# A graph network's edge work in two halves: the first half's src-ordered stage runs beside the second half's scatter

## The reference

```python
# layer 0 (row = src, col = dst)
msg = relu((x @ W_m1.T + b_m1)[row] + (x @ W_m2.T + b_m2)[col] + edge_attr @ W_me.T + b_me)   # 96 wide
msg = relu(msg @ W_net.T + b_net)
agg = segment_max(msg, row)
x   = layernorm(x + x @ W_o1.T + b_o1 + agg @ W_o2.T + b_o2)
# layer 1
h   = gelu(concat(x[src], x[dst]) @ eW1 + eb1) @ eW2 + eb2
x   = layernorm(x + x + mlp(concat(x, segment_sum(h, dst))))
```

## Time and profile before

| | us |
|---|---|
| median of 3 runs | 3815.32 (3814.55 to 3818.74) |
| profiled execution, from its first to its last instruction (span) | 2838.6 |
| median less that span | 976.7 |
| PE, PEld, DVE, ACT, POOL busy in the profiled execution | 2320.7, 2014.7, 2036.0, 1000.7, 1860.7 |

### The profile page before, as it was taken

One profiled execution on the slowest core, in us unless ns is written; L12 is line 12 of the kernel. 1 busy time (PEld: TensorE's weight loads), 2 busy tenths in 40 slices (PEclk: granted clock), 3 DMA queues, 4 the chain that ended last, 5 costly groups with the idle time before them and its releaser, 6 DMA issues. The chain is left out here.

```text
span 2838.6 us, 89638 instructions
## 1 busy us (share of the span) xinstructions
PE 2320.7 (82%) x22430; PEld 2014.7 (71%) x22431; DVE 2036.0 (72%) x9631; ACT 1000.7 (35%) x2286; POOL 1860.7 (66%) x2595
## 2 busy tenths in 40 slices
PE   7778888888888888799999988876677777777777
PEld 6578777777777777477777766766677666777777
DVE  8678777777777777777787877566666666666666
ACT  7334333333333333144444447222222222222225
POOL 1047777777777777654444437677777777777774
PEclk9789999999999999899999998899999999999999
DMA  5021111111111111188888973222222222222221
GB/s 187 29 57 47 45 45 45 45 45 45 45 45 45 45 45 48 35 218 228 226 226 225 227 194 78 54 54 54 54 54 54 53 54 54 54 55 54 55 53 46
DMA packets 582003, 236.10 MB, mean 83 GB/s; under 512 B 512256, under 2 KB 553772, under 8 KB 581676
## 3 DMA queue, kind: packets, MB, share of 16 engines
q1 hardware_dynamic: 298020, 98.53, 15.3%
q0 software_dynamic: 52736, 93.92, 11.6%
q10 hardware_dynamic: 231176, 42.79, 7.5%
HBM read 142.39 MB, written 98.65 MB: 85 GB/s over the span
## 5 line engine op out<-in xcount | busy, mean ns | idle before, releaser
L1041 POOL DMA_INDIRECT edge_in_src_order<-u,place x784 | 756.6, 965 | 259.9 <-issue 185.2
L1714 POOL DMA_INDIRECT a_rows<-src_table,idx x782 | 742.2, 949 | 248.8 <-issue 237.9
L1791 PE MATMUL ps_h<-a_rows,ident 128*128 x1664 | 237.8, 286 | 247.3 <-SPq L1723 185.4
L1791 PEld LDWEIGHTS ps_h<-a_rows,ident 128*128 128x128 f32 x1664 | 202.6, 192 | 278.9 <-issue 278.7
L1411 POOL COPY m_s<-m 128x144 f32 x832 | 234.0, 325 | 244.0 <-PE ps_pre L1458 242.9
L1831 ACT ACTIVATE h<-ps_h 128x512 f32<-128x512 f32 x208 | 124.2, 597 | 743.6 <-PE ps_h L1796 653.9
L1760 DVE TENSOR_SCALAR ohd_f<-iota_b,dloc_c 128x128 f32<-128x128 bf16 x832 | 199.1, 312 | 209.8 <-PE ps_s L1805 204.1
L1434 DVE TENSOR_TENSOR_SCAN top<-same,top,ps_net 96x512 f32<-96x512 bf16 x207 | 264.1, 1276 | 97.9 <-PE ps_net L1465 97.6
L1335 ACT COPY u<-ps_u 128x384 f32<-128x384 f32 x196 | 93.7, 478 | 604.1 <-DMA edge_in_src_order<-u,place 581.7
L1258 PE MATMUL ps_u<-we_s,attrT 128*128 128x384 f32 x392 | 173.8, 525 | 158.9 <-ACT u L1335 158.9
L1748 DVE TENSOR_TENSOR hsumT<-hsumT,ps_s 128x128 f32 x832 | 238.2, 286 | 84.4 <-DVE deg L1750 1.8
(11 more groups left out here) (357 smaller groups left out, 5400.8 us busy)
## 6 DMA issues: line engine op xcount, KB each, us to landing
u_in<-edge_in_src_order SPq DMA_DIRECT2D x208, 192.0 KB, 3.4
running_max<-row ACTq DMA_DIRECT2D x208, 192.0 KB, 4.2
rowt<-src_row SPq DMA_DIRECT2D x208, 130.0 KB, 3.7
key_b<-edge_keys ACTq DMA_DIRECT2D x832, 1.5 KB
edge_in_src_order<-u,place POOLq DMA_INDIRECT x784, 2.2
a_rows<-src_table,idx POOLq DMA_INDIRECT x782
edge_attributes<-in_edge_attr SPq DMA_DIRECT2D x8, 784.0 KB, 12.0
attr_in<-edge_attributes SPq DMA_DIRECT2D x196, 32.0 KB, 1.9
```

The source lines that it names most:

```text
L1041: pool.indirect_dma_start(u_d, bass.IndirectOffsetOnAxis(place[:, u, j:j + 1], 0), ur[:, u, j, :], None).then_inc(sent[u], 16)
L1714: pool.indirect_dma_start(a_rows[:, 4 * u + j, :], None, a_d, bass.IndirectOffsetOnAxis(idx[:, u % 4, j:j + 1], 0)).then_inc(got[u % 4], 16)
L1791: m.matmul(ps_h[k][:, j, :], ident[:], a_rows[:].rearrange("p c d -> p (c d)")[:, bass.ds(slot[j], D)], start=(j == 0), stop=False, skip_g ...
```

## The change

The edges are split into two halves of 98 groups. Each half has its own ranks and its own region of `u_d` and `s_d` (111 groups each, 222 together, where there were 208).

- **Tables block.** Only the first half's histogram is counted there (49 turns). The block borders of dst come from a search and not from 50 sign passes on ACT. `m2` is made for blocks of 112 nodes (56 of them, not 49), and its last 16 partitions hold `w_e`. The keys are no longer bounced through DRAM. The wide matmuls with ones are f16 and not f32.
- **Scatter stage.** The attributes are loaded transposed into partitions 112 to 127 of `dstT`, so that one matmul against `m2` adds the edge part: L1238 and L1258 go, and the ACT copy of the attributes with them. The 12 one-hots become 3 `tensor_tensor` operations. `ps_eq`, `ps_cnt`, `ps_pre`, `ps_net` and `ps_top` have one bank each while both stages run. The sends read a ring of 16 groups (`ring_u`, `ring_p`) in place of 4 buffers. All 200 turns are straight-line code.
- **Hooks.** The second half's histogram, both halves' marks and slot rows, the ranks of the second half, the offset tables of layer 1, and zeros for the second half of `s_d` are done at given turns of the scatter stage.
- **Turns.** From turn K0 = 98 + 16 - 4 = 110 to turn 199 each engine runs one group of the scatter stage and one of the src-ordered stage. SP waits, before the first group of each half, until all sends of that half have landed. The rest of the src-ordered stage, 132 groups, follows alone.
- **Staging.** The `m1` limbs are staged by DVE (two chunks) and ACT (two chunks) and no longer by POOL. `oh`, `m1_s`, `msg` and `top` have 2 buffers, not 4.
- **Gathers.** The last rows are gathered for each half while the stage runs (98 indirect transfers), and DVE takes the maximum of the two halves. `x1T` is overlaid by the ring and loaded again after the last send.

```diff
-def pipeline(eng, count, stages, cool=0, unroll=4):
+def pipeline(eng, last, stages, done=0, cuts=(), cool=0, unroll=4, early=8):
...
+RG = 16
...
+                GB = 2 * GS
+                K0 = CS + RG - 4
+                C_STEPS = CG + 4
+                KS = C_STEPS - K0 + 1 & -2
...
+                def pick_bank(banks, i, u):
+                    return banks[0] if isinstance(i, int) and i < KS else banks[u % 2]
...
+                        def load_u(i, u, n):
+                            if isinstance(i, int) and i in (0, GS):
+                                groups_sent(sp, CS if i == 0 else CG)
...
+                        for i in range(CG):
+                            wait(pool, sent[i % 4], 64 * (i // 4))
+                            pool.wait_ge(place_ready, i + 1)
+                            pool.wait_ge(u_ready, i + 1)
+                            for j in range(4 * (i % RG), 4 * (i % RG) + 4):
+                                pool.indirect_dma_start(u_d, bass.IndirectOffsetOnAxis(ring_p[:, j:j + 1], 0),
+                                                        ring_u[:, j, :], None).then_inc(sent[i % 4], 16)
...
+                            for table, to, size in ((lo_f, ohlo[:, u], SL), (dloc, ohd[:, i % 2], BD), (hi_f, ohhi[:, i % 2], HIW)):
+                                last = v.tensor_tensor(to, bcast(table[:, now].rearrange("p (c a j) -> p c a j", a=1, j=2), P, 2, size, 2),
+                                                       bcast(iota_2[:, 0:size].unsqueeze(1), P, 2, size, 2), ALU.is_equal)
...
+                        def stage(i, u, n):
+                            wait(dve, pre_ready, i - 1)
+                            at = offsets(nc, mybir.EngineType.DVE, sf_row[0:1, bass.ds(4 * i, 2)], (NB - 1) * 3 * F)
+                            for j in range(2):
+                                last = v.tensor_copy(m1_s[:, u % 2, j, :], m1[:, bass.ds(at[j], 3 * F)])
...
+                        order = [("d", 4, scan), ("c", 3, advance), ("c", 3, same_step), ("c", 3, coarse), ("c", 4, across_steps), ("c", 3, fine),
+                                 ("c", 4, put), ("c", 0, onehot), ("d", 0, onehot_b), ("d", 0, stage)]
...
+                        order = [("c", 1, turn), ("d", 3, net), ("c", 3, product), ("d", 5, turn_top), ("c", 3, count), ("c", 2, equal), ("d", 1, pre_u)]
...
+                        for now in range(C_STEPS):
+                            for kind, lag, work in order:
+                                step([(kind, lag, work)], kind, CG if kind == "c" else GB, now - (0 if kind == "c" else K0))
+                            hooks(now)
+                        pipeline(pe, GB, [(lag, work) for kind, lag, work in order if kind == "d"], done=C_STEPS - K0, early=KS + 4)
```

More of the change, by code:

```diff
@@ L27 @@
 C_HI, C_LO, C_DST = 0, 1, 2
+BD = 112
 CH = 7
@@ L43, in sizes @@
     return nb, q, ns
-def pipeline(eng, count, stages, cool=0, unroll=4):
+def pipeline(eng, last, stages, done=0, cuts=(), cool=0, unroll=4, early=8):
     most = max(lag for lag, _ in stages)
-    warm = most + 2 * unroll
-    warm += -warm % unroll
-    end = (count - cool) // unroll * unroll
+    ends = [0, *cuts, last]
     def turn(k, u):
@@ L58, in turn, with straight, step @@
             n, v = k + (u - lag) // unroll, (u - lag) % unroll
-            if isinstance(k, int) and not 0 <= unroll * n + v < count:
+            i = unroll * n + v
+            if isinstance(k, int) and not 0 <= i < last:
                 continue
-            stage(unroll * n + v, v, n)
-    def straight(first, last):
-        for t in range(first, last):
+            stage(i, v, n)
+    def straight(lo, hi):
+        for t in range(lo, hi):
             turn(t // unroll, t % unroll)
[L66 to L70, removed]
+    for a, b in zip(ends, ends[1:]):
+        lo = max(done, a + most + (early if a == 0 else 0))
+        lo += -lo % unroll
+        hi = (b - (cool if b == last else 0)) // unroll * unroll
+        if hi - lo < 2 * unroll:
+            continue
+        straight(done, lo)
+        with eng.Fori(lo // unroll, hi // unroll) as k:
             for u in range(unroll):
                 turn(k, u)
-    straight(end, count + most)
+        done = hi
+    straight(done, last + most)
+def step(stages, of, count, t):
+    for kind, lag, stage in stages:
+        i = t - lag
+        if kind == of and 0 <= i < count:
+            stage(i, i % 4, i // 4)
 def offsets(nc, engine, row, last):
@@ L1436, in scan, with border_rows @@
                                                  ALU.mult, ALU.max).then_inc(top_ready, 1)
-                        pipeline(dve, G, [(4, scan), (0, onehot)])
+                        def border_rows(q):
+                            wait(dve, x_turned, q - 2)
+                            for j in range(min(4, ND - 1 - 4 * q)):
+                                b = 4 * q + j + 1
+                                last = v.tensor_scalar(oh_x[:, q % 3, j, :], iota_b[:, 0:BD], split_l[:, b:b + 1], None, ALU.is_equal)
+                            last.then_inc(x_oh, 1)
@@ new lines, in _ @@
+                        order = [("d", 2, first), ("c", 1, turned), ("c", 3, rows), ("d", 5, rows_out_of), ("d", 6, store), ("d", 0, stage)]
+                        for q in range(BX):
+                            act.wait_ge(x_turned, q + 1)
+                            wait(act, x_ready, q - 1)
+                            k = min(4, ND - 1 - 4 * q)
+                            s.copy(dstT_x[:, q % 2, 0:k].rearrange("p j e -> p (j e)"), ps_split[q % 2][0:BD, 0:P * k]).then_inc(x_copied, 1)
+                        act.wait_ge(x_chain, ND)
```

2422 lines of the change are left out of this document (1312 added, 1110 removed).

## The result

The changed kernel takes 3759.8 us (median of 4 runs, 3746.5 to 3778.0) where the kernel before takes 3816.7 (4 runs, 3814.6 to 3818.7): ratio 0.9855, 95% interval 0.983 to 0.9881. That is faster, as forecast, and clear of noise, but by 57 us and not by 186, and 3760 lies above the stated range of 3530 to 3710.

What follows compares the result with a forecast made beforehand. POOL's transfers were taken to bound the scatter stage and layer 1's edges, PE the src-ordered stage. Terms -166, -30 and +10 made -186: span 2653, time 3630 us; likeliest range 3590 to 3680, wider range 3530 to 3710.

Steps and rivals of the forecast that it cites:

- the frame: Whole kernel: span 2838.6 us, median 3815.3; the 976.7 us taken as outside the span are carried over unchanged.
- Rival 4: Whole kernel: time outside the span isn't constant; 3565 us if runs slow proportionally, 3545 if sends are slower; chance 0.24.
- Tables block: Before the first send: fewer histogram turns and no key bounce gain 30 us (10 to 55), first send at 164.
- First half sent: Scatter stage: POOL finishes the first half's 98 groups 506 us after s, the first send.
- Scatter turns: Scatter stage before sharing: POOL's four sends set 5.06 us a turn, with PE at 3.15 and DVE at 2.6.
- Shared turn: Turns with one scatter and one src-ordered group: 5.8 us each (5.3 to 6.6), including a stall behind `rowt`.
- Rival 1: Shared turns: slower at 6.6 us each, 70 us more, 3700 us, but the change still gains; chance 0.17.
- Lone group: Src-ordered groups run alone after the shared turns: 2.42 us each (2.32 to 2.8), 319 us in all.
- Stage: Scatter, slot rows and src-ordered stage together: from 1504 to 1338 us after the first send, gain 166.
- Node stage: Node stage: taking the gathers out gains nothing; last store, last gather, maximum and engines' meeting add 10 us.
- Rival 2: Shared turns: DVE's port use stretches sends from 1.266 to 1.39 us and POOL bounds; 3600 to 3640 us, chance 0.13.
- Rival 3: Shared turns: over 7.9 us because PE waits for DVE's scan behind a late `rowt`; slower than before, 3865; chance 0.06.

Runs made afterwards that it cites:

- g0: Kernel before with layer 1's 782 indirect POOL gathers replaced by SyncE loads of fixed rows, on a slow chip: 3215.9 us, ratio 0.8505.
- s0: Kernel before with its scatter stage written out turn by turn on all five engines, not as a loop, on a slow chip: 3798.2 us, ratio 0.9952.
- experiment 3: Changed kernel with no shared turns (K0 = 196, not 110), on a slow chip: 3885.8 us, ratio 1.028 to the kernel before.
- a1: Changed kernel with only three waits held at 1 or more, several runs on a slow chip: 3726.4 us against 3780.9 for the kernel before, ratio 0.9866.
- experiment 6: Changed kernel with half 1's 49 node gathers each issued beside one of half 2's, not in one run, on a slow chip: 3719.4 us, ratio 0.9751.
- b0: Kernel before run again with only two waits on loaded values held at 1 or more, on a quick chip: 2838.0 us.
- a0: Changed kernel run again with only three waits on loaded values held at 1 or more, on a quick chip: 2663.0 us.
- k196: Changed kernel with K0 = 196, so the src-ordered stage starts only after all scatter groups, on a slow chip: 3885.8 us, ratio 1.028.
- m0: Changed kernel with the two halves' node gathers issued in pairs instead of 49 in one run, on a slow chip: 3719.4 us, ratio 0.9751.
- g1: Kernel before with layer 1's indirect gathers replaced by plain transfers of fixed rows, still issued by POOL, on a slow chip: 3127.9 us, ratio 0.8195.
- g2: Kernel before with two of each group's four layer 1 gathers replaced by SyncE loads of fixed rows, on a slow chip: 3152.2 us, ratio 0.8261.
- p3: m0 with a 384-wide POOL memset ahead of each layer 1 gather, on a slow chip: 3433.2 us, ratio 0.9079 to the kernel before.

## Why the prediction was wrong

**The step that failed is the frame.** The prediction says: "I make the sum in the span's time and carry the 976.7 us outside it over unchanged." Those 977 us lie inside the stages, and nearly all of them where POOL issues indirect transfers. For the kernel before on slow chips: scatter stage 1396 against 995 (g0's window), layer 1 1448 against 978, and the node stage, whose 49 gathers are one run, 142 (s0, last scan to first layer-1 gather) against 88: together some 925. The rest is spread. There was a warning: no run had given a time and a span of the same execution, and a median and a span that differ by a third need not be of like executions. With the frame fell what was read from the quick trace and carried over: a scatter turn of 5.06 us is 7.1 to 7.5 on a slow chip, and a shared turn of 5.8 is 7.9 to 8.2.

The Trainium skill, "Runtime: NRT & Kernel Launch", section "The ~15µs preamble/postamble breakdown", puts some 9 to 15 us around a kernel; that was nearer than my frame. The runs show 1.7 to 2.0 us between an execution's time and its span.

**Rival 4** was the nearest of the cases, and had the wrong victim. It priced a slower send at 977 / 1615 = 0.6 us each and concluded that PE then has more room, gain 270. It is right that the loss goes with the indirect transfers. But their own time is the same on both kinds of chip (0.95 us busy, 0.30 behind it); it is PE, DVE, ACT and SP that stand still. So PE gets no more room there: on slow chips a shared turn takes 7.9 to 8.2 us, the lighter scatter turn stays at 7.2 to 7.5, and the sharing hides 159 us (experiment 3) where the rival had 209.

**Where the gain went on a slow chip**, from g0 and a1 on one chip (first send, last src-ordered scan, end of span): before 194.4, 2108.4 and about 3779; after 141.1, 2077.4 and 3718.5. Prologue 53 us gained; the two stages 1914.0 against 1936.3, 22 lost where a quick chip gains 131; behind them 1671 against 1641, 30 gained. Together 61; the medians differ by 54.5, since a1's profiled run is its fastest. The 153 us between the 131 and the -22 lie in two places. Up to the last send the changed kernel takes 1506 us where before takes 1395, on the quick chip 1012 where before takes 993: 92, of which 34 fall in the first half's turns, lighter as they are, and 58 in the second's, most of them shared. From there to the last scan it takes 432 where before takes 521, on the quick chip 356 where before takes 507: 61, and the run of 49 gathers, which stood in the node stage before, costs about that there (experiment 6). The node stage is 51 shorter for it (142 in s0, 91 in a1).

**The sum itself**, against the quick chip (b0 and a0 together, by windows and the starts of scans):
- *Tables block, 30 forecast (10 to 55).* First send 196.5 to 141.8: 55. Undersized, at its bound.
- *First half sent at s + 506.* The 393rd send begins at s + 506.4. Right to the 4 us that I had put on top for landing and load.
- *Scatter turns, 5.06.* 5.17 us before sharing. Right: POOL's pace, DVE and PE below it.
- *Shared turn, 5.8 (5.3 to 6.6).* 76 scans in 418.5 us are 5.5 each, with PE 442 of 444 us busy, while POOL's groups go on at 5.16 from the ring's lead. PE bounds it; the stall behind `rowt` that I added is small, 14 us of waits in 390. Rival 1 is out.
- *Lone group, 2.42 (2.32 to 2.8).* 125 scans in 344.8 us are 2.76: PE is 0.91 busy and DVE 0.81, and they wait for each other. Undersized by 0.34 x 132 = 45 us, the largest error of the sum. Whether the 2 buffers in place of 4 or the staging on DVE and ACT is behind it wasn't tested. The sum also counts 87 + 21 + 111 = 219 of the 222 groups; three more at 2.42 are 7 us.
- *Stage, 166.* 1498.1 against 1366.9 from first send to last scan: 131.
- *Node stage, -10.* 86 us before, 92 after: -6.
- Sum: 55 + 131 - 6 and 5 lost in layer 1 and the last stage, 175 against 186. That they lie so close is in part luck: the tables gave 25 more than forecast and the stage 35 less.

**Rival 2** (DVE's marks and copies stretch the sends). Sends in the shared turns of the quick chip:

```profile
L1299 POOL DMA_INDIRECT edge_in_src_order<-ring_u,ring_p x303 | 298.8, 986 | 92.5 <-issue 82.1 <-DMA edge_in_src_order<-ring_u,ring_p 7.0 <-ACT ring_u L1699 1.8
```

986 ns against 963: 23 ns more and not the 128 of the earlier trace rows, and the turns before sharing show 986 too. **Rival 3** (a shared turn over 7.9) did happen, on slow chips, but not by its mechanism of a late `rowt`: PE and the others stand still; and as the kernel before is slower there too, it didn't decide the sign.

What stays open: what differs between the two kinds of chip, and that it is the chip; what in an indirect transfer holds up the other engines, and on which of them it falls first; k196 on a quick chip. It isn't the loading of code: layer 1 of s0 has 11 packets on the queues for instructions from 2300 to 3600 us, and that of b0, with no stop, 11 from 1800 to 2700. The ratio of a1 to m0 compares two slow chips, each with its own runs of before.

## What to carry to other kernels

If a profiled execution and the timed ones differ by more than a few us, find out first that they are the same thing: compare span, granted clock and stages of one execution with its own time, and make no sum before that. Where a stage issues many indirect transfers from POOL, time its kernel on several chips: a change that moves other engines' work beside such transfers was worth 6.2% on one kind and 1.4% on the other. There, runs of such transfers 1.25 us apart cost more than pauses do; with plain transfers, with pairs and a pause (1.99 us from one to the next on average), or with an even 1.58 us, layer 1 got shorter. On the quick kind the even spacing only costs: 3341 against 2838 us for the kernel before, and 3130 against 2663 for the changed one.

## What the hardware showed that I had not expected

- In five of the seven sets of runs (the result's and six more, these on six chips) PE, DVE, ACT and SP stand still while POOL issues indirect transfers one behind the other; in the other two there is hardly such a gap. The transfers themselves take 0.95 us of POOL, and their last packet ends 2.2 us after their start, on both kinds of chip. The Trainium skill, "SBUF — State Buffer", section "SBUF: two separate sides", says that compute and DMA can't slow each other ("A DMA cannot be slowed by a compute op, and vice versa"). g1's plain transfers agree with it. Beside the gathers, at the same 64 KB each, the other engines do stand still; that it happens at the SBUF isn't shown, so this needn't contradict the page, but a reader of it would not expect the stops.
- The stops come in steps. Of the pairs of L2059's weight loads that follow each other in layer 1 (after, 2300 to 3500 us), 71 begin 0.6 to 0.8 us apart, 51 begin 1.3 to 1.5 apart, 23 begin 2.1 to 2.2 apart and 27 at another distance over 0.4; on the quick chip none reaches 0.4.
- The granted clock goes with the stops: 0.74 to 0.77 in layer 1 and in the changed kernel's turns that aren't shared, 0.83 in the scatter stage of before, 0.90 in the shared turns, and 0.98 to 1.00 in layer 1 without them (g0, g1, g2, quick chips). For layer 1's same matmuls PE is busy 967 us at 0.74 and 753 at 0.99. Of the 485 us that the stage gets longer PE is thus busy for 214 and idle for 271; how much of the 485 the clock itself causes isn't shown.
- On slow chips a kernel got 7% faster (p3's 0.9079 against m0's 0.9751 of before) by 350 us of memsets on the engine that sets its pace.
